# W_lat and three bias vectors loaded from ScalarE's queue in a one-core transformer layer

## What is computed

```python
k = x @ W_lat + b_lat                                  # (2, 512, 128)
q = (x @ W_d + b_d).reshape(2, 512, 16, 128)           # 16 heads
att = softmax(causal(q @ k.T / sqrt(128)))
y = (att @ k) -> (2, 512, 2048)
x = layernorm(x + y @ W_proj + b_proj)
scores = x @ router_weight + router_bias
top 256 tokens of each sequence: h = gelu(sel @ w1 + b1) @ w2 + b2, times sigmoid(score)
out = layernorm(x + scattered h)
```

## Time and profile before

| what | value |
|---|---|
| median of 3 runs | 283.8 us (283.8 to 284.01) |
| the profiled execution | 284.02 us, of it span 282.3 us |
| TensorE busy | 273.0 us (97% of the span) |
| VectorE, ScalarE, GpSimd busy | 219.4, 210.6, 154.2 us |
| DMA | 15.53 MB, mean 55 GB/s |

### The profile page before, as it was taken

One profiled execution on the slowest core, in us unless ns is written; L12 is line 12 of the kernel. 1 busy time (PEld: TensorE's weight loads), 2 busy tenths in 40 slices (PEclk: granted clock), 3 DMA queues, 4 the chain that ended last, 5 costly groups with the idle time before them and its releaser, 6 DMA issues.

```text
span 282.3 us, 6211 instructions
## 1 busy us (share of the span) xinstructions
PE 273.0 (97%) x1885; PEld 247.3 (88%) x1885; DVE 219.4 (78%) x703; ACT 210.6 (75%) x575; POOL 154.2 (55%) x214
## 2 busy tenths in 40 slices
PE   8999999999999999989999999999999999999991
PEld 4887999999999998989999999998999999989990
DVE  2687677777777777777789888899978978769882
ACT  3688777777787778887787777787777777865481
POOL 6468444444433336555666766665657847237732
PEclk9999999999999999999999999999999999999998
DMA  6493111111111111111111111110112200020241
GB/s 192 126 305 105 40 24 35 36 37 37 33 26 34 37 38 37 39 37 42 37 37 39 37 41 37 38 39 19 37 41 76 77 21 19 3 77 0 77 137 49
DMA packets 18842, 15.53 MB, mean 55 GB/s; under 512 B 1641, under 2 KB 18178, under 8 KB 18818
## 3 DMA queue, kind: packets, MB, share of 16 engines
q1 hardware_dynamic: 18242, 13.65, 16.3%
q0 software_dynamic: 576, 1.58, 1.6%
HBM read 12.60 MB, written 2.63 MB: 54 GB/s over the span
## 4 chain that ended last, share of the span: by engine, by line
PE 89%; DVE 4%; ACT 4%; issue 2%; POOLq 0%; DVEq 0%; ACTq 0%
PE bank L403 19%; PE bank L405 17%; PE bank L404 17%; PE bank L538 8%; PE ps_out L403 6%; PE ps_out L405 6%; PE ps_out L404 6%; PE bank L597 2%; PE bank L518 2%; ACT pT_hi L804 1%; PE bank L461 1%; DVE beats L1191 1%; ACT probs L797 1%; ACT qT_hi L753 1%; DVE squared L1165 1%
## 5 line engine op out<-in xcount | busy, mean ns | idle before, releaser
L797 ACT ACTIVATE probs<-probs,negmax 128x512 f32<-128x512 f32 (+3 forms) x128 | 72.6, 575 | 6.3 <-DVE negmax L973 4.9
L1323 POOL TENSOR_TENSOR wd_hi<-wd_raw,zero 128x256 fp32r<-128x256 f32 x31 | 24.1, 779 | 89.7 <-DVE probs L1037 86.7
L804 ACT CAST pT_hi<-bank 128x512 fp32r<-128x512 f32 (+2 forms) x96 | 43.4, 488 | 28.7 <-PE bank L538 28.7
L973 DVE CUSTOM_DVE_ANT_0 probs<-bank,mask_row 128x512 f32<-128x512 f32 (+3 forms) x128 | 59.2, 482 | 0.7 <-PE bank L495 0.7
L980 DVE TENSOR_TENSOR pT_lo<-bank,pT_hi 128x512 fp32r<-128x512 f32 (+2 forms) x96 | 53.0, 553 | 7.1 <-ACT pT_hi L804 6.1
L538 PEld LDWEIGHTS bank<-ident_r,prob_words 128*128 128x128 f32 x320 | 33.9, 140 | 5.7 <-ACT probs L850 0.7
L403 PE MATMUL bank<-kT_hi,qT_hi 128*128 128x256 f32 (+2 forms) x94 | 36.5, 389 | 0.8 <-DVE kT_lo L945 0.7
L403 PE MATMUL ps_out<-wp_hi,yT_hi 128*128 128x256 f32 x124 | 37.2, 300 | 0.0
L405 PE MATMUL ps_out<-wp_hi,yT_lo 128*128 128x256 f32 x124 | 35.0, 283 | 0.0
L994 DVE TENSOR_TENSOR yT_lo<-bank,yT_hi 128x512 fp32r<-128x512 f32 x31 | 21.4, 690 | 17.5 <-PE bank L405 15.5
L404 PE MATMUL ps_out<-wp_lo,yT_hi 128*128 128x256 f32 x124 | 35.0, 282 | 0.0
(11 more groups left out here) (198 smaller groups left out, 729.7 us busy)
## 6 DMA issues: line engine op xcount, KB each, us to landing
wd_raw<-in_L_attn_W_d SPq DMA_DIRECT2D x32, 128.0 KB, 2.1
wp_raw<-in_L_attn_W_proj SPq DMA_DIRECT2D x32, 128.0 KB, 2.0
wf_raw<-in_L_ffn_w SPq DMA_DIRECT2D x2, 1024.0 KB, 7.3
x_nat<-in_L_attn_x SPq DMA_DIRECT2D x4, 256.0 KB, 2.9
out<-z_all SPq DMA_DIRECT2D x4, 256.0 KB, 2.2
picked<-ranked SPq DMA_DIRECT2D x2, 258.0 KB, 2.8
wlat_raw<-in_L_attn_W_lat SPq DMA_DIRECT2D x1, 128.0 KB, 3.5
bproj_all<-in_L_attn_b_proj SPq DMA_DIRECT2D x1, 128.0 KB, 3.2
```

Of the source, the lines that this page charges most:

```text
L797: act.activation(p_tile(s, j), p_tile(s, j), ACT.Exp, bias=negmax[:, s, j:j + 1], scale=-1.0, accum_out=sums[:, s, j:j + 1]).then_inc(exp_ ...
L804: act.copy(pT_hi[:, turns[n][3]], turns[n][2]).then_inc(pt_hi_done, 1)
L973: dve.tensor_tensor_reduce(p_tile(s, j), score_bank[j], mask_row[:, (TILES - 1 - j) * P:], -SCALE, -MASKED, ALU.add, ALU.min, accum_out=ne ...
L1323: pool.tensor_tensor(hi, src, nothing, ALU.add).then_inc(hi_done, 1)
```

## The change

Four loads move from SyncE's queue to the head of ScalarE's. What SyncE issues and in what order is otherwise as it was, and no wait and no semaphore changes.

```diff
@@ sync
             load_x(0)
-            sp.dma_start(wlat_raw[:], W_lat.rearrange("(c p) l -> p c l", p=P)).then_inc(wlat_in, 16)
             load_wd(0, 0, 0)
-            sp.dma_start(bias_rows[0:HEADS, :], b_d.rearrange("(h l) -> h l", l=LAT)).then_inc(bias_in, 16)
-            sp.dma_start(bias_rows[B_LAT:B_LAT + 1, :], b_lat.rearrange("(a l) -> a l", a=1)).then_inc(bias_in, 16)
-            sp.dma_start(bias_rows[B_ONE:B_ONE + FCH, :], b1.rearrange("(f l) -> f l", l=P)).then_inc(bias_in, 16)
             load_wd(1, 1, 1)
             load_x(1)
@@ scalar
+            act.dma_start(wlat_raw[:], W_lat.rearrange("(c p) l -> p c l", p=P)).then_inc(wlat_in, 16)
+            act.dma_start(bias_rows[0:HEADS, :], b_d.rearrange("(h l) -> h l", l=LAT)).then_inc(bias_in, 16)
+            act.dma_start(bias_rows[B_LAT:B_LAT + 1, :], b_lat.rearrange("(a l) -> a l", a=1)).then_inc(bias_in, 16)
+            act.dma_start(bias_rows[B_ONE:B_ONE + FCH, :], b1.rearrange("(f l) -> f l", l=P)).then_inc(bias_in, 16)
             x_high(0)
             act.wait_ge(wd_in[0], 16)
```

## The result

| | kernel before | changed kernel |
|---|---|---|
| median | 283.8 us (5 runs, 283.74 to 284.01) | 285.44 us (5 runs, 285.26 to 285.93) |
| profiled execution | 284.02, span 282.3 | 285.92, span 284.2 |

The ratio is 1.006 with an interval of 1.0048 to 1.0071. The forecast was 283.8, with 283.2 to 284.5 as its range: too low by 1.6 us, and the time lies outside. The profiled executions differ by 1.9 us of span. First the chain of waits of the changed kernel over its first 12 us (start us, us, what), to be read against the earlier trace rows. Its lines in the TensorE part stand four lower than those of before: L421 is L425, L423 is L427, L425 is L429, L428 is L432, L430 is L434, L432 is L436, L399 to L401 are L403 to L405, L457 the waking matmuls, L411 the transposes. (In the later runs too the same code stands a few lines higher or lower than before; the order of the pieces is the same.)

A forecast was written before the change was run, and what follows sets the result against it. TensorE, busy for 97% of the span, was taken as the bound, with loads mattering only at the ends. Terms -0.34 - 0.05 + 0.36 = -0.03 took 284.02 to 283.99, or 283.8 as median; range 283.2 to 284.5.

The forecast's parts named there:

- Carrying the front over whole: From 8.10 us on, whatever the front gains or loses reaches the end unchanged: 1 us there is 1 us at 282.3.
- Part 1: SyncE's queue: four issues of 1.52 us leave, later loads are issued earlier; gain on the path: nothing.
- Part 2: Transpose of the biases (L434): its 0.37 us idle was read as a wait for the last bias transfer; gain 0.34 us.
- Part 3: W_lat, issued at 0.80 instead of 1.80, frees L425, but L427 needs x's second cast; gain 0.05, bounds 0 and 0.27.
- Part 4: x's second half is pushed back by W_lat's 131 KB: 0.36 us lost, bounds 0 and 0.63.
- Part 5: ScalarE's head: four issues move the table load's end to 3.60, ahead of the cast at 4.84; cost 0.
- Rival D: A later x delays the rise of TensorE's clock until after the first queries: +2.5 us, 286.3; chance 0.05.
- The sum: Whole kernel: -0.34 - 0.05 + 0.36 = -0.03 us against the profiled 284.02, so 283.99; as a median 283.8.

The follow-up runs named there:

- with the gap: Kernel before with five waking matmuls for six, so TensorE stands still longer ahead of the first transpose; 285.22 us, ratio 1.0044.
- probe: Kernel before with the transpose of the biases moved ahead of the products of K, all loads on SyncE's queue; 283.81 us in one execution.
- W_lat alone: Against the kernel before, only the W_lat load moves to ScalarE's queue, the bias loads stay on SyncE's; 285.45 us, ratio 1.0063.
- 128-row tile: Kernel before with the bias rows in a cleared tile of all 128 partitions and a 128-column identity for their transpose; 283.70 us, ratio 0.9993.
- filled version: Changed kernel with one waking matmul more ahead of x's transposes and one between their halves; 284.33 us, ratio 1.0014 to the kernel before.

## Why the prediction was wrong, point by point

- **Carrying the front over whole** was right from the end of the first queries on, and not from 8.10, as the prediction had it. The end of K (L436, 8.10 before) moved by 1.55 us, to 9.65, and the span by 1.9: by its own sign ("I am wrong if anything behind 8.10 moves by another amount than L436 does") this step failed, by the 0.31 us that the queries lost to the clock. From the end of the queries in the front to the end of the span it is 272.8 or 272.9 us in five profiles: before 9.48 and 282.3, changed 11.34 and 284.2, changed again 10.91 and 283.8, with the gap 10.81 and 283.7, probe 9.22 and 282.1. In the profile of W_lat alone it is 273.2.
- **Part 1** was right: in the changed kernel's front nothing waited for the loads that moved up on SyncE's queue, and the split of unit 2, which had waited for its load before, waits for TensorE.
- **Part 2 failed.** The gain of 0.34 us did not exist. I took idle time with the releaser "issue" for a wait on a load since the code has a semaphore there. The biases alone on the other queue, the probe and the 128-row tile show that it is TensorE's own time ahead of the transpose with 25 rows. I had set no bound on that reading, and should have set one at 0.
- **Part 3** was right in kind: W_lat was early by 1.20 us, and L421's load, at 6.17, no longer waits for it; in the chains of W_lat alone and of the filled version the cast of x (L758, L757) ends ahead of this product. What it was worth can't be read off, since x had moved.
- **Part 4** was right in mechanism and mis-sized: 0.36 taken, 0.63 measured in the first profile. That this is the upper bound exactly is luck: the second profile of the changed kernel has the fifth transpose at 5.02 and W_lat alone at 5.00, so 0.72 and 0.70 behind 4.30, both beyond it. Nor did the engines run at the 207 GB/s of the earlier trace rows, as that bound supposes. They were slower from 2.5 to 3.0 us (271 for 342 GB/s), which is 35 KB fewer, and then as fast as before (365 for 363 GB/s). By estimate that is 0.36 us for W_lat's 131 KB and 0.1 for the slower stretch; where the remaining 0.2 comes from isn't shown. The Trainium skill's rule that an engine takes turns between rings ("DMA: Bandwidth & Descriptors", Queues, rings and completion order) said which end to take, and the trace agrees with it: 0.09 MB from either queue between 3.0 and 3.5 us, and W_lat's cast at 4.16, ahead of x's second half, which TensorE has at 4.93. The same page's sentence that more issuing engines save only issue time (Issuing engines are not separate DMA queues) fits too: two queues moved no more than one did (365 for 363 GB/s between 3.0 and 3.5).
- **Part 5** was right: the table load ended at 4.00, ahead of the cast at 5.47. The four issues took 1.79 us instead of 1.52, and with the gaps between them 1.89 (0.80 to 2.69).
- **Rival D, the clock**, is what decided: the sum has nothing for it, and I gave it 0.05. Its size was over-priced (2.5 forecast; 1.22 by the first profile, 0.91 + 0.31), since the rise came during the queries and not after them, and L427 (0.29 in the earlier trace rows) had partly been at the lower level before. Its chance was the real fault. I wrote that the idle time would be "about equal", reckoning that the earlier W_lat takes idle time away. It takes away none: the second pair of waking matmuls fills just that wait, 5.05 to 5.93 in the two lines above. And x's delay comes in two pieces, one before each half (0.27 and 0.34 us of idle time in the rows above). A kernel with waking matmuls in it says that its time hangs on the clock, and a change that opens a gap behind them should have had the clock as its first rival.
- **The sum** with what was measured: 0 for part 2, 0.5 to 0.6 for x (0.46 by the filled version, 0.64 by the chain), 1.1 to 1.2 for the clock (1.1 by the filled version against the changed kernel, 1.22 by the chain). That is 1.6 by the medians and 1.9 by the profiled pair, and both come out at the measured difference since they are parts of it; what the filled version adds is that the clock's part can be had back alone.

What stays open: what makes a single execution fall in the upper or the lower group, and whether doubling W_lat makes the upper one rarer. The length of the idle time alone doesn't seem to decide it, since the kernel with W_lat doubled has the longest (TensorE's matmuls stand still for 0.55 and 0.33 us ahead of the two halves) and four of its seven executions in the lower part.

## What to carry to other kernels

A load that is moved to a second queue doesn't only start earlier. Here it took turns with what the first queue had under way, which was the very thing that the front waits for: 131 KB cost x's second half 0.63 to 0.72 us, and 131 KB more another 0.46. Where the order of the loads on one queue already is the order in which they are needed, ask first what the moved one will pass. Where a kernel keeps TensorE awake with empty matmuls, price each new gap behind them by the stretch at the lower clock that it adds (1.1 to 1.35 us here, for gaps of 0.3 to 0.4), and fill the gap in the same edit. And idle time put down to "issue" isn't a wait for a load until moving the load moves it.

## What the runs showed of the hardware that I had not expected

- Where it stands between the products of K, the transpose of 25 or 26 bias rows leaves 0.35 to 0.37 us idle ahead of its operand load at the upper level of the clock (2.4 GHz), in float32 and in float32r, and 0.60 to 0.65 at the lower (1.2 GHz), in float32; widened to 128 rows and columns it leaves none.
- TensorE's clock can stay at its lower level some 3 us longer for one 512-column matmul less: 0.43 a step until 9.6 instead of about 6.5, in a kernel with the same transfers. The profile's column for the granted clock says 1.00 all along, in the earlier trace rows and in the changed kernel's stretches in the section on the result, 7.50 to 8.00 among them; only the steps show it. The Trainium skill ("TensorE: Matmul & The Clock Gate", Part 1) says that a gate sets the rate by how busy the array has been of late; the run with the gap (285.22) and the filled one (284.33) agree.
- The same kernel has executions in two groups some 1.2 us apart beside each other: 3 and 11 of the changed kernel's 14. The upper group has a late rise of the clock in both of its profiles; that the lower one has an early rise is read from the run of W_lat alone and the filled version.
- The load of one bias row took ScalarE's queue 0.53 us to issue, 0.56 in the run of the biases alone, and SyncE's 0.32; the other three took 0.51, 0.47 and 0.28 on ScalarE's and 0.46, 0.47 and 0.27 on SyncE's.
